# Norms, constants, one late unit and roundings in another order around the first attention's way through DRAM

## What is computed

```python
# L0: attention with feature maps, then a feed-forward layer on rounded values ("quantised")
x = x + tanh(g_xattn[0]) * L0_xattn(_layernorm(x), ctx, ctx, ...)     # out @ dense_w + dense_b, layernorm
x = x + tanh(g_ffn[0])   * L0_ffn(_layernorm(x), w_gate, w_up, w_down)
# _bitlinear: _act_quant(x) rounds each row to 127 / max|x|, _weight_quant(w) rounds to -1, 0, 1
# L1: windowed attention with rotated keys (apply_rope), then 16 experts and a shared one
x = x + tanh(g_xattn[1]) * L1_xattn(_layernorm(x), ctx, ctx, ...)
x = x + tanh(g_ffn[1])   * L1_ffn(_layernorm(x), ...)
# L2: the context asks, latents are normalised x; keys are divided by their length per head
kv = concatenate([layer_norm(ctx), latents]) @ Wkv; k = l2norm(k) * k_scale; q = l2norm(q) * q_scale
x = x + tanh(g_xattn[2]) * L2_xattn(ctx, _layernorm(x), mask, ...)
x = x + tanh(g_ffn[2])   * L2_ffn(_layernorm(x), w1, b1, w2, b2, gamma, beta)   # quantised, gelu
# L3: attention over the context (keys and values from ctx @ Wk.T, ctx @ Wv.T), then 8 experts
x = x + tanh(g_xattn[3]) * L3_xattn(ctx, ctx, _layernorm(x), ...)
x = x + tanh(g_ffn[3])   * L3_ffn(_layernorm(x), ...)
```

## Time and profile before

| | us |
|---|---|
| median of 3 runs (835.27 to 838.87) | 837.63 |
| the profiled execution's own time | 838.38 |
| its span | 836.6 |
| TensorE busy | 747.0 |
| VectorE busy | 605.0 |
| ScalarE busy | 416.7 |
| GpSimd busy | 321.8 |
| granted TensorE clock, mean | 0.943 |

### The profile page before, as it was taken

How to read it: one execution, slowest core, us unless ns; L and a number is a source line. 1 busy time by engine, 2 the same in 40 slices (tenths; PEclk the granted TensorE clock), 3 DMA queues, 4 the chain that set the end, 5 groups by cost and what they waited for, 6 DMA issues and landing times.

```text
span 836.6 us, 15735 instructions
## 1 busy us (share of the span) xinstructions
PE 747.0 (89%) x5624; PEld 490.0 (59%) x5624; DVE 605.0 (72%) x1279; ACT 416.7 (50%) x694; POOL 321.8 (38%) x263
## 2 busy tenths in 40 slices
PE   4699999997876969998999999997799998998997
PEld 3577777875544565653455555563246665655575
DVE  4789999998887665557556665568789997535653
ACT  2666666676664524435554545411137776834331
POOL 0665555551423602530778777721251211100111
PEclk9999999999988868999999999998869999998999
DMA  7266766432415312216033322027715667000320
GB/s 204 74 211 244 256 215 214 167 117 94 76 50 175 118 35 81 81 39 165 2 91 108 107 77 77 0 30 109 157 54 107 129 143 151 3 1 26 112 77 24
DMA packets 50338, 87.84 MB, mean 105 GB/s; under 512 B 17386, under 2 KB 34730, under 8 KB 49922
## 3 DMA queue, kind: packets, MB, share of 16 engines
q1 hardware_dynamic: 50274, 86.98, 38.0%
HBM read 61.45 MB, written 25.51 MB: 104 GB/s over the span
## 4 chain that ended last, share of the span: by engine, by line
PE 47%; DVE 37%; ACT 5%; POOL 5%; issue 4%; DMA 1%; SPq 0%; DVEq 0%; POOLq 0%; ACTq 0%
DVE arena L2414 9%; PE ps L1145 8%; PE ps L1135 6%; DVE arena L1810 6%; DVE rn L1962 5%; PE ps L1313 3%; PE ps L1066 3%; DVE arena L2011 3%; PE ps L1323 3%; DVE arena L1990 2%; PE ps L1250 2%; PE ps L750 2%; PE ps L1239 2%; PE ps L1079 2%; DVE arena L1970 2%
## 5 line engine op out<-in xcount | busy, mean ns | idle before, releaser
L1810 DVE TENSOR_TENSOR arena<-ps,arena 128x448 f32<-128x448 f32 (+7 forms) x139 | 82.4, 617 | 57.1 <-ACT arena L1622 20.9
L2414 DVE TENSOR_REDUCE arena<-ps 112x1 f32<-112x500 f32 x192 | 114.6, 669 | 8.8 <-PE ps L1222 8.7
L1747 POOL TENSOR_TENSOR arena<-arena 125x448 f32<-125x448 f32 x96 | 109.2, 1138 | 24.6 <-ACT arena L1567 20.8
L1145 PE MATMUL ps<-arena 125*128 125x448 f32 (+1 forms) x208 | 97.2, 548 | 2.0 <-ACT arena L1567 1.5
L1598 ACT ACTIVATE arena<-ps 125x896 f32<-125x896 f32 x96 | 87.2, 917 | 22.7 <-PE ps L1239 22.7
L1567 ACT ACTIVATE arena<-arena,kbias 125x448 f32<-125x448 f32 x96 | 63.6, 668 | 65.4 <-DVE arena L1810 47.9
L1810 DVE TENSOR_TENSOR arena<-ps,rn 125x448 f32<-125x448 f32 x96 | 59.2, 618 | 48.8 <-PE ps L1135 43.9
L1135 PE MATMUL ps<-arena 128*125 128x448 f16 (+3 forms) x312 | 76.6, 354 | 0.1
L825 PE MATMUL ps<-w_k2h,arena 128*125 128x512 f16 x288 | 67.6, 386 | 8.5 <-ACT arena L1379 8.5
L1135 PEld LDWEIGHTS ps<-arena 128*125 128x125 f16 (+1 forms) x312 | 40.3, 133 | 53.7 <-issue 42.3
L1725 POOL TENSOR_TENSOR arena<-arena 112x512 f32<-112x512 f32 x23 | 29.1, 1267 | 88.9 <-DVE arena L1810 88.7
(11 more groups left out here) (310 smaller groups left out, 1413.8 us busy)
## 6 DMA issues: line engine op xcount, KB each, us to landing
arena<-in_ctxT SPq DMA_DIRECT2D x8, 750.0 KB, 9.4
d_cln<-arena SPq DMA_DIRECT2D x8, 750.0 KB
d_clnT<-arena SPq DMA_DIRECT2D x8, 750.0 KB
d_k<-arena SPq DMA_DIRECT2D x24, 250.0 KB
d_v<-arena SPq DMA_DIRECT2D x24, 250.0 KB
arena<-d_clnT SPq DMA_DIRECT2D x8, 750.0 KB
arena<-in_ctx SPq DMA_DIRECT2D x8, 672.0 KB
arena<-d_cln SPq DMA_DIRECT2D x8, 672.0 KB
```

Of the source, the lines that this page charges most:

```text
L1145: pe.matmul(ps[0:D, 4 + 2 * p, 0:N], cln_s[p][0:rows, t, :], pexp[(t + p) % 2][0:rows], start=(t == 0), stop=(t == KT)).then_inc(l2_pv, 1)
L1747: ins = pool.tensor_tensor(psum2[p][0:rows], psum2[p][0:rows], pexp[(t + p) % 2][0:rows], ALU.add)
L1810: return dve.tensor_tensor(out, a, b, op)
L2414: dve.tensor_reduce(mx3[bn % 2][:, u % 2, u % 8 // 2, u // 8:u // 8 + 1], ps[0:TT, max_bank_of(bn, u), 0:500], AX.X, ALU.max).then_inc(l3_ ...
```

## The change

Nothing is computed in another way, only in another order and partly by another engine:

- TensorE: unit 11 is made behind the dense product of y2 and two more key tiles. Ahead of the transposes of y2 stand ten tiles of keys and not twelve; behind the dense product two, unit 11 and six.
- ScalarE: unit 10 and k1T come ahead of the constants, which now stand behind twelve squares; unit 11 behind them. The root of the key norms stands behind units 17 and 18. Gelu's matmuls are preceded by the constants of v3s, which GpSimd set before.
- VectorE: of the key rotation only the product with sink is left (GpSimd multiplies by cosk and adds). The rounding of three weight matrices stands behind the copy of y2, the key biases far later. Norms 4 and 5 stand in the second norm's wait for its root, 6 to 8 as before, 9 in the tail, 10 and 11 behind the copy of the second attention's x, and the limit of all norms behind the query's bias.
- GpSimd: the remainder of unit 11 stands behind two roots, the key blocks wait for the context's stores themselves.
- SP: the loads of units 20 to 23 stand behind the stores of units 16 to 18.
- Latents: three of four key sums move ahead of the copies of qT2, the reciprocal into the middle of the eight subtractions.
- keep_clock: 26 to 22, 14 to 7, 12 to 6.

```diff
--- before.py
+++ after.py
@@ -612,10 +613,11 @@
                 store_later(u)
-            sp.wait_ge(rn_sq, 1)
-            for u in range(20, 24):
-                load_later(u)
             for u in range(16, 24):
+                if u == 19:
+                    sp.wait_ge(rn_sq, 1)
+                    for v in range(20, 24):
+                        load_later(v)
                 store_later(u)
@@ -906,15 +908,16 @@
             pe.matmul(ps[0:D, 0, 0:N], cs("rot"), k1T, start=True, stop=True).then_inc(l1_kv, 1)
-            later(11)
             pe.wait_ge(l0_att, 3)
             l2_keys(B - 1, 0, 8, range(KT // 2, KT), bank=3)
-            l2_keys(B, 1, 0, range(KT // 2), bank=3)
+            l2_keys(B, 1, 0, range(4), bank=3)
             pe.wait_ge(l0_ld, 32)
...
             by_tokens(xT2, w_d0[:, :], 0)
-            l2_keys(B, 1, 0, range(KT // 2, KT), bank=3)
+            l2_keys(B, 1, 0, range(4, 6), bank=3)
+            later(11)
+            l2_keys(B, 1, 0, range(6, KT), bank=3)
@@ -948,7 +951,7 @@
                 else:
-                    keep_clock(26, 7)
+                    keep_clock(22, 7)
@@ -1021,6 +1024,7 @@
+            pe.wait_ge(l1_zero, 3)
             scores1(0)
@@ -1098,7 +1102,7 @@
             mm.then_inc(l2_m, 1)
-            keep_clock(14, 3)
+            keep_clock(7, 3)
             op.next()
@@ -1123,7 +1127,7 @@
             op.next()
-            keep_clock(12, 2)
+            keep_clock(6, 2)
             op.next()
@@ -1447,6 +1451,11 @@
             act.copy(kvt[:, 4:B, :].rearrange("p b n -> p (b n)"), ps[0:D, 1, :]).then_inc(l0_kvt, 1)
+            later(10)
+            act.wait_ge(l1_kv, 1)
+            act.activation(k1T, ps[0:D, 1, 0:N], ACT.Identity, bias=w_col1[:, 1:2]).then_inc(l1_ak, 1)
+            l2_squares(B - 1, 8, range(KT // 2, KT), bank=3)
+            l2_squares(B, 0, range(6), bank=3)
             for p in range(2):
@@ -1460,12 +1469,8 @@
                          ones[rows].unsqueeze(2).broadcast_to([S, 64, 1])).then_inc(l1_zero, 1)
-            later(10)
-            act.wait_ge(l1_kv, 1)
-            act.activation(k1T, ps[0:D, 1, 0:N], ACT.Identity, bias=w_col1[:, 1:2]).then_inc(l1_ak, 1)
             later(11)
-            l2_squares(B - 1, 8, range(KT // 2, KT), bank=3)
-            l2_squares(B, 0, bank=3)
+            l2_squares(B, 0, range(6, KT), bank=3)
             act.wait_ge(l1_zero, 5)
@@ -1481,10 +1486,11 @@
             later(14, 15, 16)
+            later(17, 18)
             act.wait_ge(rn_sq, 1)
...
             act.activation(rn_flat, rn_flat, ACT.Sqrt).then_inc(rn_sd, 1)
-            later(17, 18, 19)
+            later(19)
             act.activation(qss[0:1, 2, 0:1], tg[0:1, 0:1], ACT.Exp)
@@ -1568,6 +1574,16 @@
+            act.wait_ge(l3_free, 1)
+            for p in range(2):
+                act.activation(v3s[p].rearrange("p j n -> p (j n)"), ones[0:KP].broadcast_to([KP, KT * 192]),
+                               ACT.Identity, scale=0.0).then_inc(l3_vz, 1)
+            act.wait_ge(l3_vz, 2)
+            for p in range(2):
+                act.copy(v3s[p][:, :, 0:D].rearrange("p j (g c) -> p j g c", c=32)[:, :, :, 24:25],
+                         ones[0:KP].unsqueeze(2).unsqueeze(3).broadcast_to([KP, KT, 4, 1]))
+                act.copy(v3s[p][:, :, D:].rearrange("p j (g c) -> p j g c", c=16)[:, :, :, HD16:HD16 + 1],
+                         ones[0:KP].unsqueeze(2).unsqueeze(3).broadcast_to([KP, KT, 4, 1])).then_inc(l3_vz, 1)
             for t in range(NT):
@@ -1691,7 +1707,11 @@
-            remainders(10, 11)
+            remainders(10)
+            pool.wait_ge(l1_kv, 2)
+            ch.link(pool.tensor_tensor(k1T, k1T, cs("cosk"), ALU.mult))
+            pool.wait_ge(l1_k, 1)
+            pool.tensor_tensor(k1T, k1T, xT3, ALU.add).then_inc(l1_k, 1)
@@ -1704,12 +1724,14 @@
-            pool.wait_ge(l1_zero, 3)
-            pool.wait_ge(l1_k, 1)
+            for p in range(2):
+                pool.wait_ge(st[p], 32 * (B // 2 + 1))
+            pool.wait_ge(l1_k, 2)
             key_blocks(0)
...
             rsqrt()
+            remainders(11)
             remainders(12, 13, 14, 15, 16)
@@ -1749,11 +1771,6 @@
             rsqrt()
-            for p in range(2):
-                ch.link(pool.memset(v3s[p], 0.0))
-                ch.step(pool.memset(v3s[p][:, :, 0:D].rearrange("p j (g c) -> p j g c", c=32)[:, :, :, 24:25], 1.0))
-                ch.step(pool.memset(v3s[p][:, :, D:].rearrange("p j (g c) -> p j g c", c=16)[:, :, :, HD16:HD16 + 1], 1.0))
-            ch.sync()
             rsqrt()
@@ -1780,6 +1797,7 @@
             pool.wait_ge(l3_free, 2)
+            pool.wait_ge(l3_vz, 4)
             pool.wait_ge(l3_q, 1)
@@ -1820,7 +1838,7 @@
-            def layernorm(src, dst, eps, gain=None, bias=None, twice=False):
+            def layernorm(src, dst, eps, gain=None, bias=None, twice=False, meanwhile=None):
@@ -1837,6 +1855,8 @@
                     ch.sync()
+                if meanwhile:
+                    meanwhile()
                 rstd_in.next()
@@ -2100,18 +2120,15 @@
                 ins.then_inc(l0_att, 1)
-            quantised_weights(slice(0, 3))
             dve.wait_ge(l1_kv, 2)
-            ch.step(tt(xT3, ps[0:D, 0, 0:N], cs("sink"), ALU.mult))
-            ch.link(tt(k1T, k1T, cs("cosk"), ALU.mult))
-            tt(k1T, k1T, xT3, ALU.add).then_inc(l1_k, 1)
+            tt(xT3, ps[0:D, 0, 0:N], cs("sink"), ALU.mult).then_inc(l1_k, 1)
             ch.step(dve.memset(q1T[:, N:N + 8], 0.0))
...
             l2_norms(B - 1, 8, range(KT // 2, KT))
-            l2_norms(B, 0, range(KT // 2))
+            l2_norms(B, 0, range(4))
             turned(xT2, 2)
-            key_biases()
+            quantised_weights(slice(0, 3))
             product_in.next()
@@ -2121,11 +2138,12 @@
                 dve.wait_ge(st[p], 32 * (B // 2 + 1))
-            layernorm(x, z, 1e-5)
+            layernorm(x, z, 1e-5, meanwhile=lambda: l2_norms(B, 0, range(4, 6)))
+            dve.wait_ge(lv_full, 11 - IN_TURNS + 1)
             quantise(z, y, zq, ((2, 0), (3, 1)))
...
             dve.tensor_copy(zqT, ps[0:D, 0, 0:256].bitcast(BF16)[:, 0:N]).then_inc(operand, 1)
-            l2_norms(B, 0, range(KT // 2, 9))
+            l2_norms(B, 0, range(6, 9))
             for t in range(NT):
@@ -2150,20 +2168,22 @@
             quantise(big2, big3, hq, ((4, 2),), ffn=0)
-            l2_norms(B, 0, range(9, KT))
+            l2_norms(B, 0, range(9, 10))
+            down(4)
+            residual(4, y)
+
+
+            layernorm(x, z, 1e-5)
+            signal(operand)
+            turned(xT, 0)
+            l2_norms(B, 0, range(10, KT))
+            product_in.next()
+            q1 = q1T[:, 0:N]
+            dve.tensor_scalar(q1, ps[0:D, 1, 0:N], w_col1[:, 0:1], None, ALU.add).then_inc(operand, 1)
             dve.wait_ge(sq_used, KT * B + SQ)
...
             dve.tensor_scalar(rn_flat, rn_flat, 1e-24, None, ALU.max).then_inc(rn_sq, 1)
-            down(4)
-            residual(4, y)
-
-
-            layernorm(x, z, 1e-5)
-            signal(operand)
-            turned(xT, 0)
-            product_in.next()
-            q1 = q1T[:, 0:N]
-            dve.tensor_scalar(q1, ps[0:D, 1, 0:N], w_col1[:, 0:1], None, ALU.add).then_inc(operand, 1)
+            key_biases()
             product_in.next()
@@ -2311,22 +2331,34 @@
                    over(qss[:, 2, H8 * t:H8 * t + H8], [TT, H8, HD8]), ALU.mult).then_inc(operand, 1)
+            def latent_key_sums(t):
+                act_in.next()
+                ch.step(dve.tensor_reduce(qss[:, 1, H8 * t:H8 * t + H8],
+                                          big3[:, t, :].rearrange("p (h d) -> p h d", h=H8), AX.X, ALU.add))
+
+            def latent_key_sums_last():
+                ch.link(dve.tensor_reduce(qss[:, 1, H8 * (NT - 1):], big3[:, NT - 1, :].rearrange("p (h d) -> p h d", h=H8),
+                                          AX.X, ALU.add))
+                dve.tensor_scalar(qss[:, 1, :], qss[:, 1, :], 1e-24, None, ALU.max).then_inc(to_act, 1)
+
+            for t in range(NT - 1):
+                latent_key_sums(t)
             product_in.next(3)
...
                 ch.step(dve.tensor_copy(qT2[:, :, TT * t:TT * t + TT], ps[0:D, t, 0:N].rearrange("p (c n) -> p c n", c=4)))
-            act_in.next(5)
+            act_in.next(2)
             signal(operand)
-            ch.link(dve.tensor_reduce(qss[:, 1, :], big3.rearrange("p t (h d) -> p (t h) d", h=H8), AX.X, ALU.add))
-            dve.tensor_scalar(qss[:, 1, :], qss[:, 1, :], 1e-24, None, ALU.max).then_inc(to_act, 1)
-            act_in.next()
-            dve.reciprocal(qss[:, 1, :], qss[:, 1, :]).then_inc(l2_kn, 1)
+            latent_key_sums_last()
             for h in range(H8):
...
                 ch.step(tt(qtT[:, 1, h, :], ps[0:D, h, 0:N], qtT[:, 0, h, :], ALU.subtract))
-                if h % 4 == 3:
+                if h == 3:
                     signal(operand)
+                    act_in.next()
```

(2 more changed lines are left out.)

7 lines of the change are left out of this document (4 added, 3 removed).

## The result

The changed kernel takes 832.16 us (median of 14 runs, 829.23 to 837.01), the kernel before 838.33 in the same comparison (14 runs). The ratio of the two kernels' runs is 0.9937, 95% interval 0.9918 to 0.9957: 5.3 us faster (3.6 to 6.9). The direction was right and the time lies inside the range, but the gain is about half of what was forecast. Its profiled execution took 833.87 us, with a span of 832.1 (before 836.6).

The account below looks back on a forecast made before the run. Bound: the chain through VectorE's twelve key norms, not the DRAM round trip. 3.3 + 1.7 + 2.2 + 2.0 + 0.5 = 9.7 us off 838.38 gives 828.7, 828.0 as median; range 823.5 to 833.0.

Parts of the forecast that it names:

- Part 1: First attention's way through DRAM: dense product of y2 starts 4.9 us earlier, the addition behind it 4.7 us.
- GpSimd was in the way: Rival, chance 0.20: GpSimd's key blocks delay VectorE's casts, norms and dense product by 1.7 us; 830.4 us with a low clock.
- Part 2: From the dense product to the first Silu: ScalarE's row takes some back; 3.3 us of 5.2 kept.
- ScalarE and not VectorE would be the bound: Behind the dense product ScalarE limits up to the v1 copies; the rival, VectorE as bound, chance 0.15, gave 826 us.
- Part 3: Norms out of the tail behind the hidden tiles' rounding: one norm stays, 1.7 us won, second attention 5.0 us earlier.
- Part 4: Latents ahead of the third attention: fewer clock-keeping matmuls 1.4 us, reordered key sums and fewer keepers 0.8; together 2.2 us.
- the second half: Latents: three key sums ahead of the copies, 6 keepers for 12: 0.3 to 1.6 us, 0.8 taken.
- Part 5: Second quantised layer: v3s' constants moved to ScalarE shorten VectorE's scales, 2.0 us; 26 keepers cut to 22, 0.5 us.
- A low clock goes: Rival, chance 0.08: one of TensorE's later low-clock stretches falls away by luck, 4 us more: 824 us.
- Part 2 gives all back: Rival, chance 0.09: ScalarE's row takes the 3.3 us and the following 1.7; 3.9 us remain, 833.7 us.
- The loads of units 20 to 23: Slower rival, chance 0.03: these loads, waiting for the maximum of all norms, hold TensorE up at unit 20; 843 us if landing at 289.
- The marks named for being wrong: v1 copies after 236, casts ending after 216, unit 20 waiting for its load, or third attention less than 6 us earlier.

Follow-up runs that it names:

- b_latents: Kernel before with the latents' change alone (key sums ahead of copies, 14 keepers cut to 7, 12 to 6): ratio 1.002 to before.
- a_keep_z: Changed kernel with 12 keepers ahead of the turning of z alone: ratio 0.9919 to the kernel before.
- a_const_clock: Changed kernel with ScalarE's constants ahead of the squares of tiles 4 and 5, plus 27 keepers around y2, rounded tiles and z: ratio 0.992 to before.
- a_best: a_const_clock with key sums behind the copies, 7 and 12 keepers in the latents, 15 for 6 ahead of the experts: 827.53 us, ratio 0.9889 to before.
- b_early: Kernel before with parts 1 to 3 of the change alone: ratio 0.9987 to before.
- a_no_latents: Changed kernel without part 4 (sums behind the copies, 14 and 12 keepers again): ratio 0.9942 to the kernel before.
- a_one_keeper: a_no_latents with 7 in place of 14 keepers ahead of the latents' transposes: ratio 0.994 to the kernel before.
- a_const_early: Changed kernel with ScalarE's constants ahead of the squares of tiles 4 and 5, no added keepers: ratio 0.9933 to the kernel before.

## Why the prediction was right in direction and wrong in size

- **Part 1, right.** 4.9 us at the dense product; 4.4 measured (4.3 to 4.5 in eleven executions of that order; 3.3 in three, where the first keys ran at the low clock). The round trip through DRAM now ends TensorE's wait (in the three, the norms still do). The casts are not held up by the key blocks; GpSimd was in the way elsewhere, where its rival did not look, with unit 10's remainder (0.4 us).
- **Part 2, term mis-sized.** 3.3 us taken; 3.0 in the profiled execution, but 1.2 to 3.0, in the mean 2.1, over nine executions of this order without keepers ahead of y2. The step that failed: the key tiles ahead of and behind the dense product were priced at the full clock, with 1.2 and 0.7 us of idle time just opened in front of either; in six of the nine they ran low. That ScalarE and not VectorE would be the bound was right.
- **Part 3, failed.** 1.7 us taken, none left at the experts' end (0.1 in the profiled execution). VectorE did win 1.4 of it up to the down scaling. In front, GpSimd's remainder beside a small instruction took 0.5. Behind, TensorE waited 3.5 us instead of 2.2 for z and did the turning and the first product at the low clock (0.7 us, of which 0.55 are left at the first scores; the second product ran low before, too), and 0.3 more went up to the experts' end, where nothing names the cause. The prediction looked for GpSimd's remainders only behind the root and counted nothing; the earlier trace rows show the same kind of instruction at 0.17 and at 2.22 us, so that its place beside any remainder had to be asked for.
- **Part 4, failed most.** 2.2 us taken; 0.9 lost in the profiled execution, 0.2 won in the mean of the executions, 1.7 lost in the runs of `b_latents`, nothing in those of the changed kernel. The first half, 1.4 us for seven fewer keepers, is right where the clock is low there (1.35) and nothing where it is not. In the second half the prediction saw the idle time of 2.6 us and chose the low clock, but let it act on the six keepers alone. It also acts on the sixteen matmuls (+2.9 us here, +1.5 to 1.7 in five of nine executions), and, in some executions, on the third attention's first batch (+2.4). The upper bound of 1.6 us was no better: with the clock held in both orders the new one is worth 0.1. It had compared the new order at the full clock with twelve keepers at the low one (4.38 us), which take 2.76 at the full.
- **Part 5, right.** 2.0 us taken, 2.05 measured in every kernel that has it. (In the earlier trace rows VectorE's instruction begins 0.17 us ahead of the memset that holds it up; which of the two was issued first those rows do not show.) The 0.5 us for four fewer keepers did not show: the stretch takes 25.4 to 26.5 us with 22 and 25.4 to 26.4 with 26.
- **The rivals.** "A low clock goes" had the mechanism with the opposite sign: here one came. "Part 2 gives all back" named 3.9 us; nearer to 5.3 than the forecast, but by another way. The loads of units 20 to 23 held nobody up in the changed kernel; where keepers brought z forward, TensorE did wait for one of them (0.78 us in `a_keep_z`, 0.64 in `a_const_clock`, 0.74 in `a_best`), so that sign was near.
- **The marks named for being wrong.** The third attention came less than 6 us earlier (392.59 against 396.19: 3.6; 4.5 from the end of the context pass): that mark spoke rightly. The v1 copies came after 236 (236.45), and the casts ended after 216 (216.17), only because this execution was 0.9 us late at the end of the context pass. Those marks were passed by chance, and should have been given from there.

## What to carry to other kernels

A saving that opens an idle time in front of TensorE is not finished when the idle time is there: price everything that TensorE does behind it at the low clock as well, and either fill the gap with matmuls that end before the operand comes or count the loss. Cheap work that must stand somewhere goes into the idle time in front of a wait, not behind it: 2.5 us of constants moved by two instructions' places gave 1.6 us. And where the clock makes stages come out in two ways, one profile is one draw: the same order gave 1.2 to 3.0 us at one mark and a loss or a gain at another, so sizes are read from several executions, marks are counted from a common point ahead of the change, and a gain that is gone later is followed to the idle time where it went.

## What the runs showed of the hardware

- The granted clock fell behind idle times of 1.2 and 0.7 us in a row in four of the seven executions that have them without keepers around y2's transposes (`b_early`, `a_no_latents`, `a_one_keeper`, `a_const_early`), and behind 0.7 and 1.2 us ahead of the first keys in three of fourteen. It fell behind 2.28 us ahead of the latents' products in eight of nine; behind 0.79 us in front of the same products it fell in none of seven.
- Ahead of the experts the length of the idle time tells what follows: eight matmuls take 3.25 us behind 1.6 to 2.2 us of it (twelve executions), 4.95 behind 2.3 to 2.4 (three) and 6.2 behind 2.55 (two).
- Keepers cost by the clock, not by their number alone: the same 12 in the same place, behind 2.38 us of idle time, took 4.38 us in the earlier trace rows and 2.76 in `a_best`.
- A gain in clock at one place did not add up: with z's keepers the first scores came 2.2 us earlier in the kernel before, 2.1 of them were left when z was turned for the experts, and behind the longer idle time there (2.55 us, 1.90 before) the experts ended 1.1 us later than without the keepers. Whether the keepers lengthen that idle time, or it was chance, was not settled; with the same keepers it was 1.67 in `a_const_clock`.
- VectorE and GpSimd stretch each other: three of VectorE's tensor_scalars took 1.67 us in place of 1.28 and GpSimd's remainder beside them 1.48 in place of 1.07.
